# Macaron block, 16-head relative attention: normalisation moved into each head, output projection in blocks, value products moved behind the last batch and into head 0

## What is computed

```python
q, k, val = heads(x @ Wq + bq), heads(x @ Wk + bk), heads(x @ Wv + bv)
content_score = einsum('bhsp,bhtp->bhst', q + u, k)
pos_score = relative_shift(einsum('bhsp,htp->bhst', q + v, pos))
weights = softmax((content_score + pos_score) / sqrt(8), axis=-1)
out = einsum('bhst,bhtp->bhsp', weights, val)
return out.transpose(0, 2, 1, 3).reshape(B, S, D) @ Wo + bo
```

## Time and profile before

| | us |
|---|---|
| three runs | 441.93, 442.1, 444.17 |
| median | 442.1 |
| the profiled execution, its own time | 440.37 |
| its span in the trace | 438.2 |
| first row maximum of head 0 starts | 89.53 |
| last transpose of head 15 starts | 378.38 |
| first addition of the attention to `x` starts | 391.79 |

### The profile page before, as it was taken

How to read it: one execution, slowest core, us unless ns; L and a number is a source line. 1 busy time by engine, 2 the same in 40 slices (tenths; PEclk the granted TensorE clock), 3 DMA queues, 4 the chain that set the end, 5 groups by cost and what they waited for, 6 DMA issues and landing times.

```text
span 438.2 us, 18062 instructions
## 1 busy us (share of the span) xinstructions
PE 352.7 (80%) x7328; PEld 285.1 (65%) x7328; DVE 398.4 (91%) x579; ACT 264.2 (60%) x650; POOL 122.0 (28%) x172
## 2 busy tenths in 40 slices
PE   1878798786988989879898798887988989677774
PEld 1557566674766767668677577675776767673564
DVE  8888986389999999999999999999999999947785
ACT  1668365356666666666666666666666666514980
POOL 7445656646022020220202202012020120025652
PEclk9989998999999999999999999999999999886998
DMA  7004267484132321322313223132131302400002
...
DMA packets 58884, 30.67 MB, mean 70 GB/s; under 512 B 35486, under 2 KB 57598, under 8 KB 58718
## 3 DMA queue, kind: packets, MB, share of 16 engines
...
q10 hardware_dynamic: 672, 0.80, 0.6%
...
## 4 chain that ended last, share of the span: by engine, by line
DVE 61%; issue 18%; PE 8%; ACT 6%; POOL 3%; SPq 2%; DVEq 1%; DMA 0%; POOLq 0%; ACTq 0%
DVE pT L944 31%; DVE negmax L930 20%; ACT v_rep L646 2%; DVE xh L751 2%; PE pair L1064 2%; ACT v_rep L634 1%; DVE v_rep L869 1%; DVE sqsum L863 1%; PE pair L1019 1%; DVE stat L741 1%; DVE x L877 1%; ACT xT L606 1%; PE pair L1235 1%; SPq L332 1%; PE pair L1133 1%
## 5 line engine op out<-in xcount | busy, mean ns | idle before, releaser
L682 ACT ACTIVATE probs<-pair,negmax 128x512 f32<-128x512 f32 x256 | 173.9, 684 | 106.5 <-DVE negmax L930 106.5
L944 DVE STREAM_TRANSPOSE pT<-probs 128x1024 f32<-128x1024 f32 x128 | 156.8, 1225 | 0.5 <-ACT probs L682 0.5
L930 DVE TENSOR_REDUCE negmax<-pair 128x2 f32<-128x1024 f32 x128 | 151.7, 1185 | 5.7 <-PE pair L1183 5.7
L1166 PE MATMUL pair<-stage_k,stage_c 128*32 128x512 f16 x1024 | 116.1, 404 | 44.8 <-ACT probs L682 41.6
L1172 PE MATMUL pair<-stage_z,stage_q 128*32 128x512 f16 x1024 | 110.3, 381 | 0.0
L1183 PE MATMUL pair<-stage_z,stage_q 128*32 128x222 f16 (+57 forms) x1024 | 102.1, 280 | 0.0
L549 POOL COPY v_diag<-v_rep 32x512 f32 (+1 forms) x64 | 39.0, 609 | 219.7 <-PE pair L1198 212.3
L1178 PE MATMUL pair<-stage_z,stage_q 128*32 128x8 f16 (+57 forms) x1024 | 97.1, 275 | 0.0
L1198 PE MATMUL pair<-pT,v_diag 128*32 128x128 f32 (+1 forms) x2176 | 93.2, 272 | 3.6 <-DVE pT L944 3.6
L1166 PEld LDWEIGHTS pair<-stage_k,stage_c 128*32 128x32 f16 x1024 | 49.7, 140 | 67.2 <-ACT probs L682 56.5
L1198 PEld LDWEIGHTS pair<-pT,v_diag 128*32 128x32 f32 x2176 | 73.6, 115 | 4.1 <-DVE pT L944 3.8
...
## 6 DMA issues: line engine op xcount, KB each, us to landing
...
```

The costliest lines, as they stand in the source:

```text
L682: nc.scalar.activation(probs[:, q % 6, :], score_pair(q // 2)[:, q % 2, :], ACT.Exp, bias=negmax[:, q % 8:q % 8 + 1], accum_out=rowsum[:, ...
L930: nc.vector.tensor_reduce(negmax[:, 2 * n % 8:2 * n % 8 + 2], score_pair(n)[:, :, :], AX.X, ALU.max, negate=True).then_inc(max_ready, 1)
L944: nc.vector.transpose(pT[:, par, 2 * n:2 * n + 2, :].rearrange("p a s -> p (a s)"), probs[:, 2 * n % 6:2 * n % 6 + 2, :].rearrange("p a s ...
L1166: mm(bank[32 * j:32 * j + 32, :], all_rows[:, 32 * j:32 * j + 32], stage_k[:, par, :], start=True, stop=False, skip_group_check=True)
```

## The change

- **End.** Each head is normalised by itself. POOL takes the reciprocal of the head's 16 columns of row sums as a power of -1 (`widen_recip`), widens it to 128 columns, and PE spreads it over the partitions with a constant matrix, into the bank next to the head's values (`spread_recip`). ACT copies both (256 columns), POOL multiplies them (`normalise`) into `o_sb`. Heads 0 to 13 still go through scratch memory; heads 14 and 15 are multiplied straight from `o_sb` by a block form of `Wo` (`direct`). `x` is added from four banks. DVE's and PE's work on the reciprocals of all heads is gone.
- **Between FFN and heads.** Batches 2 and 3 go through transposes, `q`, `k` one behind the other; the value groups 0 to 11 come behind them, 12 to 15 between the score tiles of head 0. `mean_squares` stands one step later in both FFNs, behind the output tile. ACT's copy of a transposed batch stands behind the high halves of the batch before.
- **POOL.** It spreads head 0's values behind head 1's query loads, since now all value groups come later.

The diff, cut:

```diff
-XHAT1_STEPS = {12: 0, 16: 1, 19: 2, 22: 3}
-TURN1_STEPS = {14: 0, 18: 1, 20: 2, 23: 3}
-QK_STEPS = {17: 0, 20: 1, 22: 2, 24: 3}
-QK_BANKS = ((0, 1), (0, 1), (4, 5), (0, 1))
+MOMENT_STEPS = ({8: 0, 12: 1, 16: 2, 18: 3}, {8: 0, 12: 1, 16: 2, 20: 3})
+X_STEPS = ({9: 0, 13: 1, 17: 2, 19: 3}, {9: 0, 13: 1, 17: 2, 21: 3})
+XHAT1_STEPS = {12: 0, 16: 1, 20: 2, 21: 3}
+TURN1_STEPS = {14: 0, 18: 1, 21: 2, 22: 3}
+QK_STEPS = {17: 0, 20: 1, 23: 2, 24: 3}
+QK_BANKS = ((0, 1), (2, 3), (4, 5), (0, 1))
 VW = S + S // NI
 V_GROUPS = 4 * B
-V_EARLY = 6
+V_HEAD = 12
+V_DVE = (5, 7, 9, 11)
+V_ACT = tuple(m for m in range(V_GROUPS) if m not in V_DVE)
+V_TILES = {8: 12, 10: 13, 12: 14, 14: 15}
...
+WO_BANKS = (6, 7, 4, 2)
+BOUNCED = H - 2
...
         def v_bank(n):
 
-            return 2 + n % 2 if n < V_EARLY else 2 + (n - V_EARLY) % 4
+            return 4 + n % 2 if n >= V_HEAD else 2 + n % 4
 
         def v_groups(step):
 
-            early = [k + 1 for k in QK_STEPS if QK_STEPS[k] < B - 1]
-            if step in early:
-                return range(2 * early.index(step), 2 * early.index(step) + 2)
-            return range(V_EARLY, V_GROUPS) if step - 1 in QK_STEPS else ()
+            return range(V_HEAD) if QK_STEPS.get(step) == B - 1 else ()
...
-            for h in (H - 4, H - 3):
-                send_o(h, h % 2)
-            for par in range(2):
...
+            for half in ((0, H - 4), (H - 4, H - 2)):
+                for h in range(*half):
+                    if h >= H - 4:
+                        send_o(h, h % 2)
+                for par in range(2):
+                    sp.wait_ge(o_out[par], 16 * (half[1] // 2))
+                for h in range(*half):
+                    read_o(h)
+            sp.wait_ge(av_ready, H - 1)
+            sp.dma_start(pTf[:, 0:1024], wo_blocks_d).then_inc(wo_blocks_in, 16)
...
                             .then_inc(s["x_const"], 1)
-                    g = (n - 8) // 4
-                    if n % 4 == 0 and 0 <= g < B:
+                    g = MOMENT_STEPS[f].get(n)
+                    if g is not None:
...
 
             nc.gpsimd.memset(v_diag[:, 1, :, :, :], 0.0).then_inc(v_diag_zero, 1)
             pool.wait_ge(v_diag_zero, 2)
-            for par in range(2):
-                pool.wait_ge(v_copied[par], V_GROUPS // 2)
-            spread_v(0, 0)
             pool.wait_ge(q_out, 16 * 3 * B)
             stage_queries(pool, 1, 1, staged_second)
+            for par in range(2):
+                pool.wait_ge(v_copied[par], len((V_ACT, V_DVE)[par]))
+            spread_v(0, 0)
             spread_v(1, 1)
...
                 nc.gpsimd.tensor_tensor(part, part, rep_ap(bo_row, [(0, 4), (1, D)]), ALU.add)\
                     .then_inc(x_bo, 1)
             pool.wait_ge(x_bo, B)
-            with pool.Fori(0, (H - 2) // 2) as it:
+
+            def widen_recip(h):
+
+                pool.wait_ge(probs_ready, h * NQ + NQ)
+                if not (isinstance(h, int) and h == 0):
+                    pool.wait_ge(av_ready, h)
+                nc.gpsimd.tensor_tensor(recip, rowsum[:, bass.ds(h * NQ, NQ)], minus_one, ALU.pow).then_inc(recip_ready, 1)
+                pool.wait_ge(recip_ready, h + 1)
+                nc.gpsimd.tensor_tensor(recip_wide.rearrange("p (q i) -> p q i", q=NQ),
+                                        rep_ap(recip, [(1, NQ), (0, NI)]), rep_ap(spread_mask, [(0, NQ), (1, NI)]),
+                                        ALU.mult).then_inc(recip_wide_ready, 1)
+
+            def normalise(h, par, pair):
+
+                pool.wait_ge(o_ready, h + 1)
+                pool.wait_ge(v_diag_ready, min(h + 3, H) * 4 if isinstance(h, int) else h * 4 + 12)
+                if not (isinstance(h, int) and h < 2):
+                    pool.wait_ge(o_out[par], pair * 16)
+                nc.gpsimd.tensor_tensor(o_sb[:, par, :], o_raw[:, par, 0:128], o_raw[:, par, 128:256], ALU.mult)\
+                    .then_inc(o_norm, 1)
+
+            pool.wait_ge(spread_in, 16)
+            nc.gpsimd.memset(minus_one, -1.0).then_inc(minus_one_set, 1)
+            pool.wait_ge(minus_one_set, 1)
+            widen_recip(0)
...
+            with pool.Fori(0, (H - 4) // 2) as it:
                 for k in range(2):
-                    pool.wait_ge(av_ready, it * 2 + (k + 1))
-                    spread_v(it * 2 + (2 + k), k)
+                    pool.wait_ge(av_ready, it * 2 + (3 + k))
+                    spread_v(it * 2 + (4 + k), k)
+                    normalise(it * 2 + (2 + k), k, it + 1)
+                    widen_recip(it * 2 + (4 + k))
+            normalise(H - 2, 0, H // 2 - 1)
             pool.wait_ge(v_diag_ready, 4 * H)
...
-                    if n in TURN1_STEPS:
-                        ln_evac(1, TURN1_STEPS[n])
                     if n - 1 in QK_STEPS:
                         q_high_halves(QK_STEPS[n - 1])
                         k_high_half(QK_STEPS[n - 1])
...
                     for m in v_groups(n - 1):
-                        if m % 2 == 0:
-                            act.wait_ge(v_mm, m + 1)
-                            nc.scalar.activation(v_tiles(m), ps[v_bank(m)], ACT.Copy).then_inc(v_copied[0], 1)
+                        if m in V_ACT:
+                            copy_values(m)
+                    if n in TURN1_STEPS:
+                        ln_evac(1, TURN1_STEPS[n])
...
                 act.wait_ge(av_ready, h + 1)
                 if not (isinstance(h, int) and h < 2):
-                    act.wait_ge(o_out[par], pair * 16)
-                nc.scalar.activation(o_sb[:, par, :], ps[4 + par][:, 0:128], ACT.Copy).then_inc(o_ready, 1)
-
-            for h in range(2):
-                for q in range(NQ):
-                    exp_tile(h, q)
+                    act.wait_ge(o_norm, h - 1)
+                nc.scalar.activation(o_raw[:, par, :], ps[4 + par][:, 0:256], ACT.Copy).then_inc(o_ready, 1)
+
+            for q in range(NQ):
+                exp_tile(0, q)
+                if q - 1 in V_TILES:
+                    copy_values(V_TILES[q - 1])
+            for q in range(NQ):
...
+                    if q == 3:
+                        take_o(h - 2, h % 2)
+                    if q == 11 and h == H - 1:
+                        take_o(H - 2, 0)
...
             nc.scalar.activation(gelu_b1, b1c, ACT.Gelu)
-            take_o(H - 1, 1, H // 2 - 1)
...
+            act.wait_ge(last_recip_mm, 1)
+            act.wait_ge(o_norm, H - 2)
+            nc.scalar.activation(o_raw[:, 1, 128:256], ps[0][:, 0:128], ACT.Copy).then_inc(last_recip_out, 1)
             ln_evac(2, 0)
...
-            dve.wait_ge(rec_out, 8)
-            scale_attention(0)
-            scale_attention(2)
+            dve.wait_ge(last_recip_out, 1)
+            dve.wait_ge(o_out[1], 16 * (H // 2 - 1))
+            dve.wait_ge(av_ready, H)
+            nc.vector.tensor_tensor(o_sb[:, 1, :], ps[5][:, 0:128], o_raw[:, 1, 128:256], ALU.mult)\
+                .then_inc(o_norm_last, 1)
...
-                    if n % 4 == 3 and 7 <= n < 4 * B + 3:
-                        mean_squares(s, (n - 7) // 4)
                     t = n - 5
...
-                        if t == 4:
-
-                            if f == 0:
-                                pe.wait_ge(pos_f, 1)
-                            else:
-                                pe.wait_ge(x_attn, B)
+                        if t == 4 and f == 0:
+                            pe.wait_ge(pos_f, 1)
...
                         ins.then_inc(s["ffn"], 1)
-                    if n == 4 * B + 4:
-                        mean_squares(s, B - 1)
+                    if n % 4 == 0 and n >= 8 and n < 4 * B + 8:
+                        mean_squares(s, (n - 8) // 4)
...
+            def spread_recip(h, dst):
...
+                pe.wait_ge(recip_wide_ready, h + 1)
+                return mm(dst, spread, recip_wide, start=True, stop=True, skip_group_check=True)
...
             def values(h, par, kb, q0=0, q1=NQ):
...
                         pe.wait_ge(o_ready, h - 1)
+                    if q0 == 0 and q1 == NQ:
+                        spread_recip(h, ps[4 + par][:, 128:256])
...
                 for q in range(NQ):
                     scores(h, par, q)
+                    if first and q in V_TILES:
+                        v_product(V_TILES[q])
...
+                else:
+                    pe.wait_ge(probs_ready, (H - 1) * NQ + (12, 12, 0, 15)[b])
+                for t in range(4):
+                    mm(ps[WO_BANKS[b]][:, t * 128:(t + 1) * 128],
+                       attnT[rows, b * S + t * 128:b * S + (t + 1) * 128], wo_sb[rows, :],
+                       start=t == 0, stop=False, skip_group_check=True)
+
+            def direct(h, b):
+                part = slice(32 * b, 32 * b + 32)
+                return mm(ps[WO_BANKS[b]], o_sb[part, h % 2, :], wo_blocks[part, h % 2, :], start=False,
+                          stop=h == H - 1, skip_group_check=True)
+
+            pe.wait_ge(wo_blocks_in, 16)
+            pe.wait_ge(o_norm, H - 1)
```

(17 more changed lines are left out.)

176 lines of the change are left out of this document (87 added, 89 removed).

## The result

The changed kernel takes 448.74 us in the median (446.95 to 449.93 in four runs), the kernel before 442.62 in the same session: a ratio of 1.013, with a 95% interval from 1.0085 to 1.0175. It is slower, by about 6 us. Ratios and their intervals compare the fast executions of two kernels alone: an execution more than 1.5% above the fastest of its kernel is left out of them, as two of run 1 are, its profiled one among them. The profiled execution took 448.77 and spans 447.0, against 438.2 of span before. The two spans lie 8.8 us apart and not 6, since the profiled execution before, 440.37, is 2.2 us under the median of its kernel.

The account below looks back on a forecast made before the run. DVE, with 61% of the chain, was taken to bound the kernel. Span 438.2 - 4.3 + 0.5 + 11.3 - 2.6 - 1.5 = 441.6, 3.4 more; added to the median of 442.1 this gave 445.5 us, range 438.5 to 452.

Parts of the forecast that it names:

- the third rival: All heads: a power above about 4.3 us makes POOL gate each of 14 heads, 452.5 us; chance 0.12.
- Head 0's reciprocal, 11.3 us: Head 1: PE waits for POOL's copies, additions, power (3.5 us) and widening, so a row maximum starts late; 11.3 us lost.
- Between FFN and head 0, 4.3 us gained: Before the first row maximum: value groups leave the chain and the last load lands earlier; 4.3 us gained (3 to 5.6).
- the walk through the queues: Before head 0: last load landing between 82.2 and 83.5 instead of 86.53, 3.0 to 4.4 us earlier, 3.8 taken.
- The walk of PE's value groups: Before head 0: twelve groups at 0.89 us each from about 69 end near 81.7, hidden by the loads.
- First FFN, 1.2 us: First FFN: PE's wait for split squares is covered by moving work a step later; 1.2 us gained (0 to 2.2).
- Inside head 0, 0.5 us: Head 0: groups 14 and 15 wait for ACT's copies of 12 and 13; about 0.5 us lost (0 to 1).
- Other heads, nothing lost: From head 1 on: the new path takes 4.1 us, under the 4.9 at which a row maximum waits; nothing lost.
- End, 2.6 us: Last transpose to first addition: 2.6 us gained; 5.1 with the power at 1.0, 0 with direct products one by one.
- Second FFN, 1.5 us: Second FFN: the output tile goes ahead of the split squares' wait; 1.5 us gained (0 to 2.8).
- the power does not go with columns: Rival on POOL's power, head 0's path and the end: 1.0 us instead of 3.5, giving 440.6 us; chance 0.27.
- nobody waiting in head 1: Rival: POOL's copies and additions not ahead of the reciprocal in effect, so the 11.3 us fall away, 434.2; chance 0.08.

Follow-up runs that it names:

- run 1: Changed kernel with the four additions of `bo` onto `x` moved behind head 0's widening on POOL; 445.21 us, ratio 1.003.
- run 2: Changed kernel with head 1's spreading and the additions of `bo` both moved behind head 0's reciprocal on POOL; 442.67 us, ratio 1.0009.
- run 7: Changed kernel with POOL's power on 8 of 16 columns, the other 8 reciprocals left out; one execution, 444.86 us.
- run 8: Changed kernel with head 0's reciprocal first on POOL, late value groups four score tiles earlier, keys of batches 0 and 1 behind head 0's loads; 434.46 us, ratio 0.9789.
- Run 4: Changed kernel with the writes of the keys of batches 0 and 1 moved behind head 0's loads; 446.52 us, ratio 1.0082.
- run 3: Changed kernel with the mean squares back at their old place in the first FFN alone; 448.13 us, ratio 1.0107.
- run 6: Changed kernel with the mean squares back at their old place in the second FFN alone; one execution, 451.64 us.

## Why the prediction was right, and where it was not

The forecast (slower, 445.5, between 438.5 and 452) held, but by one term that was right and large, and over one that was wrong by 6 us. Partly that is luck. The span was missed by 5.4 us (447.0 instead of 441.6), the time by 3.2 only (448.74 instead of 445.5): the prediction added its 3.4 us to the median, and that lies 1.7 above the execution whose trace it had read. The time also fell into the band of the third rival, 448 and more, though its mechanism, waits in every head, did not occur.

- **Head 0's reciprocal, 11.3 us: right**, in place, cause and size: 10.89 and 0.38 more behind it. The row maximum came 35.7 us after the first (127.03 - 91.31), 36.0 were predicted. The power was over-priced by 0.6 (2.90 instead of 3.5), the way from the widening to the row maximum took 2.8 instead of 2.4 (127.03 - 124.21). Runs 1, 2, 7 and 8 took the sum apart. The rule of the Trainium skill ("GPSIMD Engine Reference", section 3.1), 2.6 cycles an element, had left the power at 1.0; the trace does not agree.
- **Between FFN and head 0, 4.3 us gained: wrong**, by 6.1. The step that failed is the walk through the queues, "the last load landing between 82.2 and 83.5". It has the last batch extended at 73.6 and the last load landing some 8.7 us behind that, which is what 77.81 to 86.53 took before: it moved SP's issues with the batch that they waited for and gave the writes ahead of them no time of transfer. (From 77.81 on SP has ten issues up to that load, not twelve; this changes nothing here.) In the trace the DMA engines are full from 62 to 78, and SP's issues stretch with them; the last batch came 0.8 us earlier (extended at 74.9 instead of 75.7), and SP got to it as late as before. The windows before had shown 90 to 95% for these engines from 70 to 78, and the prediction did not look at them. The walk of PE's value groups was short too: they were to end near 81.7 and ended at 85.0 (82.4 to 83.9 in the other runs), so that here PE would have held the start by itself. Run 4 took a megabyte away and found 2.9 of the 4.3 us (86.59 instead of 89.53), 1.2 of them by the clock; its last load landed at 84.9, not by 83.5. The start of the profiled execution, 91.31, is the latest of six with that code; over the six the mean is 89.8, which is no gain either.
- **First FFN, 1.2 us (a part of that): wrong.** ACT's idle 2.20 us are gone, but `x` of group 0 is as late, 38.64. These are DVE's addition and POOL's root of group 0 in the changed kernel, POOL first:

```profile
33.66 1.26 POOL L505 TENSOR_TENSOR v_rep<-xT,v_rep 128x512 f16<-128x512 f32 x1 [3.99 <-ACT xT L654]
36.73 0.61 POOL L528 TENSOR_SCALAR grs<-gvar 128x4 f32<-128x4 f32 x1 [1.81 <-DVE gvar L906]
```

```profile
33.82 1.65 DVE L917 TENSOR_TENSOR sqsum<-sqsum,v_rep 128x512 f32<-128x512 f32 x1
```

  With the work earlier, POOL's subtraction falls beside DVE's addition, which takes 1.65 us instead of 0.69 (run 3, the old place, where the two do not overlap); the moments behind it are later by that, and POOL's root now waits for them. The predicted path moved, and the engine that was not on it gave the time back.
- **Inside head 0, 0.5 us: right only where the late value groups have the upper clock** (0.7 in the changed kernel's profile). Where they have the lower one, in runs 1 to 3, it is 3.1 to 3.3, above the bound of 1. The prediction had reckoned the four groups at 0.89 us each; where the clock falls to 0.50 they take twice that, with score tiles that do so too.
- **Other heads, nothing lost: right.** No row maximum of heads 2 to 15 waits in any run; with the power at 2.9 the path there is 3.5 us, under the 4.9 that it may take.
- **End, 2.6 us: right** (3.1). The direct products run side by side, 1.14 us; the Trainium skill ("TensorEngine Tiling (Array Packing)", Tiling Modes) has row tiles independent, and the trace agrees. Where the clock falls behind PE's wait of 2.6 us, 12.1 us and a gain of 1.3 are left; the prediction's lower bound of nothing had another reason, products one by one.
- **Second FFN, 1.5 us: right** (1.8), and run 6 gives it to the place of the mean squares alone.
- **The rivals.** That the power does not go with columns falls with 2.90 us; nobody waiting in head 1 falls with the row at 127.03; POOL gating every head falls with steady heads.

By the prediction's own signs, "a start of head 0 later than 84 would say that SP's queue, not the value groups, set it": head 0 began at 88.43, and that was the reading.
